# A four-layer graph network on one core: edge records padded to 72 values, degree one-hots built in pieces with waits, and one of the sorts without a wait at each operation

## The reference, cut to what matters

```python
edge_index = jnp.stack([src, dst])
h = jnp.maximum(_layernorm(x, axis=-1), 0.0)
x = x + _L0_gnn_ref(h, edge_index_t, ...)                  # attention over both directions of each edge
h = jnp.maximum(_layernorm(x, axis=-1), 0.0)
x = x + _L1_gnn_ref(h, edge_attr_64, ..., edge_index)      # two mean layers; also the mean of edge_attr_64 per node
h = jnp.maximum(_layernorm(x, axis=-1), 0.0)
x = x + _L2_gnn_ref(h, src, dst, ...)                      # mean over neighbours
h = jnp.maximum(_layernorm(x, axis=-1), 0.0)
x = x + _L3_gnn_ref(h, edge_index, ...)                    # attention with 8 heads
```

```python
deg = jax.ops.segment_sum(jnp.ones((src.shape[0],), h_e.dtype), dst, num_segments=n)
inv_deg = (1.0 / jnp.maximum(deg, 1.0))[:, None]
nbr_r = jax.ops.segment_sum(h_r, dst, num_segments=n) * inv_deg
```

## Time and profile before

| | us |
|---|---|
| median of 3 runs | 7473.32 (7467.55 to 7474.53) |
| the profiled execution | 7467.53 |
| its span | 7465.8 |
| DVE busy | 4758.9 (64%) |
| POOL busy | 4419.4 (59%) |
| PE busy | 2966.4 (40%) |
| ACT busy | 1296.9 (17%) |

### The profile page before, as it was taken

How to read it: one execution, slowest core, us unless ns; L and a number is a source line. 1 busy time by engine, 2 the same in 40 slices (tenths; PEclk the granted TensorE clock), 3 DMA queues, 4 the chain that set the end, 5 groups by cost and what they waited for, 6 DMA issues and landing times.

```text
span 7465.8 us, 65693 instructions
## 1 busy us (share of the span) xinstructions
PE 2966.4 (40%) x14101; PEld 2001.3 (27%) x14102; DVE 4758.9 (64%) x7439; ACT 1296.9 (17%) x4662; POOL 4419.4 (59%) x4260
## 2 busy tenths in 40 slices
PE   1841010110322222222222215766766467777664
PEld 0631000110212121212121213454544223233224
DVE  7998889981777777777777753333344154554544
ACT  0000000000100000000000000000000277777761
POOL 0887778887777777777777750000000477777741
PEclk6555555555555555555555556666666588888885
DMA  6112222111222222222222212424233122222211
GB/s 241 24 36 39 45 57 39 30 31 37 68 62 66 64 66 64 65 65 66 64 68 62 68 37 82 141 83 140 90 127 124 20 59 53 53 59 52 58 44 42
DMA packets 445364, 501.74 MB, mean 67 GB/s; under 512 B 233700, under 2 KB 250404, under 8 KB 440958
## 3 DMA queue, kind: packets, MB, share of 16 engines
q1 hardware_dynamic: 177882, 285.81, 11.4%
q0 software_dynamic: 140016, 139.81, 10.5%
q10 hardware_dynamic: 127284, 74.37, 3.4%
HBM read 330.98 MB, written 167.83 MB: 67 GB/s over the span
## 4 chain that ended last, share of the span: by engine, by line
POOL 54%; issue 21%; PE 13%; DVE 7%; DMA 4%; DVEq 0%; POOLq 0%; ACT 0%; ACTq 0%; SPq 0%
POOL arena L617 39%; POOL rec_dram L585 12%; PE acc L1666 9%; DVE arena L1313 2%; DMA V<-in_edge_attr_dram 2%; PE acc L1510 2%; POOL pdum L579 1%; DMA rec_dram<-V,rowst 1%; PE acc L1512 1%; POOL own_dram L603 1%; POOL arena L636 1%; PE acc L1690 0%; PE pt L1500 0%; DVE OHX L1150 0%; DVE arena L834 0%
## 5 line engine op out<-in xcount | busy, mean ns | idle before, releaser
L617 POOL DMA_INDIRECT arena<-tab_dram,jst x2976 | 2965.5, 996 | 893.6 <-issue 893.6
L585 POOL DMA_INDIRECT rec_dram<-V,rowst x800 | 1180.5, 1476 | 253.3 <-issue 245.5
L579 POOL TENSOR_TENSOR pdum<-pdum 128x1 f32<-128x1 f32 x308 | 116.2, 377 | 1698.0 <-DVE arena L1341 1363.6
L1666 PE MATMUL acc<-V,oh 128*128 x4464 | 726.0, 325 | 374.4 <-DVE arena L1313 275.3
L1313 DVE TENSOR_TENSOR arena<-arena,acc 128x192 f32 x1116 | 395.1, 354 | 639.4 <-PE acc L1666 623.3
L1666 PEld LDWEIGHTS acc<-V,oh 128*128 128x128 bf16 x4464 | 493.9, 111 | 605.9 <-issue 463.1
L745 ACT ACTIVATE arena<-arena,ew 128x64 f32<-128x64 f32 x1984 | 479.8, 333 | 88.1 <-PE acc L1690 44.3
L1150 DVE TENSOR_TENSOR OHX<-iotab,OHX 128x1024 bf16<-128x1024 bf16 x372 | 455.1, 1223 | 49.5 <-DVE OHX L1150 20.2
L745 ACT ACTIVATE OHX<-arena,ew 128x64 f32<-128x64 f32 x1984 | 479.6, 333 | 3.0
L1622 PE MATMUL pt<-OHX 128*128 128x128 bf16 x744 | 96.2, 310 | 955.4 <-DVE OHX L1150 955.4
L1622 PE MATMUL pw<-OHX 128*128 128x128 bf16 x744 | 96.1, 310 | 923.8 <-DVE OHX L1150 923.8
(11 more groups left out here) (464 smaller groups left out, 6410.3 us busy)
## 6 DMA issues: line engine op xcount, KB each, us to landing
oh<-mt_dram SPq DMA_DIRECT2D x279, 512.0 KB, 3.3
arena<-tab_dram,jst POOLq DMA_INDIRECT x2976, 2.5
mt_dram<-oh ACTq DMA_DIRECT2D x186, 256.0 KB, 2.1
rec_dram<-V SPq DMA_DIRECT2D x2, 15860.0 KB, 67.3
OHX<-rec_dram SPq DMA_DIRECT2D x122, 260.0 KB, 3.3
V<-in_edge_attr_dram ACTq DMA_DIRECT2D x100, 250.0 KB
rows_dram<-V SPq DMA_DIRECT2D x16, 1056.0 KB, 4.3
rows_dram<-arena SPq DMA_DIRECT2D x15, 1056.0 KB, 4.2
```

The costliest lines, as they stand in the source:

```text
L579: nc.gpsimd.tensor_tensor(pdum[:, 1:2], pdum[:, 0:1], pdum[:, 0:1], ALU.add).then_inc(S["pd"], 1)
L585: gp.indirect_dma_start(rec[:, :], bass.IndirectOffsetOnAxis(ap=rowst[:, q, k:k + 1], axis=0), recst[:, q, k, :], None).then_inc(S[f"scat{ ...
L617: gp.indirect_dma_start(hd.G[:, a.r, j, :], None, table[:, :], row_of(jst[:, a.r, j:j + 1])).then_inc(S[f"{x}g{a.r}"], 16)
L1666: last = nc.tensor.matmul(group_sum(g), mring[:, slot, g * 4 + k, :], hsp[:, bass.ds(rows[g * 4 + k] * (3 * D), 3 * D)], start=k == 0, sto ...
```

## The change

Three edits. First, a record has 72 values in place of 65. The seven more are set to 0 in the staging buffers once; the blank records get -1 in all eight values behind the 64. Second, `degree_ones` builds the wide one-hot in two halves of 125x1024, and the engine waits for each operation before it issues the next; there are six in place of four for a step. Third, `compare` keeps the wait between its operations for the two sorts on `SBL` only; in the sort on `SB_` one wait at the end of a step is left.

```diff
-REC = D + 1
+REC = 72
...
+            gp.memset(recst[:, :, :, D + 1:REC], 0.0).then_inc(S["blank"], 1)
...
             def degree_ones(i, q, first):
 
-                c = bass.ds((i * 2 + q) * KP, KP)
                 if not first:
                     v.wait_ge(S["dgm"], i * 2 + q - 1)
+                part = [0]
+
+                def ones_of(o, values, wide, a, n):
+
+                    k = bass.ds((i * 2 + q) * KP + a, n)
+                    V.tensor_tensor(o[:, a:a + n], iota[0:EP, 0:wide].unsqueeze(1).to_broadcast([EP, n, wide]),
+                                    values[:, k].unsqueeze(2).to_broadcast([EP, n, wide]), ALU.is_equal).then_inc(S["dg"], 1)
+                    part[0] += 1
+                    v.wait_ge(S["dg"], i * 12 + q * 6 + part[0])
                 for l in range(2):
-                    for o, k, wide in ((dhi, bkf, NC), (dlo, lof, P)):
-                        V.tensor_tensor(o[:, q, l], iota[0:EP, 0:wide].unsqueeze(1).to_broadcast([EP, KP, wide]),
-                                        k[l][:, c].unsqueeze(2).to_broadcast([EP, KP, wide]), ALU.is_equal).then_inc(S["dg"], 1)
+                    ones_of(dhi[:, q, l], bkf[l], NC, 0, KP)
+                    ones_of(dlo[:, q, l], lof[l], P, 0, KP // 2)
+                    ones_of(dlo[:, q, l], lof[l], P, KP // 2, KP // 2)
...
                     V.tensor_tensor(halves(dst, 0, 0), halves(src, 0, 0), halves(src, 1, 0), ALU.min).then_inc(S["v"], 1)
                     n[0] += 1
-                    v.wait_ge(S["v"], n[0])
+                    if bufs is SBL:
+                        v.wait_ge(S["v"], n[0])
                     V.tensor_tensor(halves(dst, 1, 0), halves(src, 0, 0), halves(src, 1, 0), ALU.max).then_inc(S["v"], 1)
...
                             V.tensor_tensor(o[r], a[r], b[r], op).then_inc(S["v"], 1)
                             n[0] += 1
-                            v.wait_ge(S["v"], n[0])
+                            if bufs is SBL:
+                                v.wait_ge(S["v"], n[0])
...
-                                RG[:, c.r, :, D:REC].to_broadcast([P, GT, P]), ALU.is_equal).then_inc(S["roh"], 1)
+                                RG[:, c.r, :, D:D + 1].to_broadcast([P, GT, P]), ALU.is_equal).then_inc(S["roh"], 1)
...
-                pe.wait_ge(S["dg"], 8 * i + 4 * q + 4)
+                pe.wait_ge(S["dg"], 12 * i + 6 * q + 6)
```

More of the change, by code:

```diff
@@ L197, in build @@
         MS = [OHXf[:, a:a + NBL * MW].rearrange("p (g x) -> p g x", x=MW) for a in (2048, 4400)]
-        lcol = V3f[:, 2200:2200 + 8 * RP]
+        lcol = V3f[:, 2304:2304 + 8 * RP]
         Dg = OHXf[0:NC, 4400:4400 + NFIL]
@@ L572, in _ @@
             gp.memset(ZF, 0.0).then_inc(S["zf"], 1)
+            gp.wait_ge(S["blank"], 3)
             gp.wait_ge(S["fill"], 16 * 2)
```

## The result

The changed kernel takes 7397.44 us (median of 4, 7395.53 to 7406.59) against 7471.79 for the kernel before (7467.55 to 7474.53, with one more run than the table above): ratio 0.9903, 95% interval 0.9886 to 0.9921. The forecast was 7418, in a range of 7375 to 7455. The profiled execution, at 7406.59, is the slowest of its four, so its gain of 61 us is smaller than the 74 of the medians.

What follows compares the result with a forecast made beforehand. The end of POOL's record scatter, paced by DVE's operations, bounds the start. DVE's +79 and -41 us are hidden, records cost 0, the scatter's end moves -55: 7473.3 - 55 = 7418 us, range 7375 to 7455.

Steps and rivals of the forecast that it cites:

- What bounds the start: Start of the kernel: everything behind 1740 us moves with the end of POOL's record scatter; DVE has 114 us of slack.
- Degree one-hots on DVE: Degree stretch: halves of 1.21 us with gaps of 0.14 take 350 us instead of 271, DVE +79 us.
- Degree one-hots on POOL: Scatters beside the degree one-hots: 178 by the end of the stretch, formerly 90.
- with holds, 1.96: Degree stretch: time for each scatter including holds, 1.96 us instead of 3.01; without holds 1.71 instead of 2.69.
- the prediction's rules: Scatter meeting a DVE operation: held until that operation ends, then needs 1.06 us; next starts 0.30 later. Unmet: 1.19.
- step by step procedure: Scatters stepped through DVE's operations: scatter end 1679.7 us, kernel before 1735.0, one-hots alone 1641.7, sort alone 1753.6.
- Sort on SB_: Sort without inner waits: DVE -41 us, ending at 1715; scatters 2.00 us each in first steps, then 2.21, formerly 1.68 and 2.17.
- the own rows: Between last scatter and first gather: 73.1 us of own rows and first loads, taken as unedited and unchanged.
- Lockout: Sort on SB_: DVE without waits keeps POOL out until the next wait; scatter end 1775, total 7510 us; chance 0.08.
- Missed gap: Degree stretch: scatters miss the 0.14 us gap, so 136 pass, not 178; scatter end 1758, total 7492 us; chance 0.07.
- Width: Record scatter: row width sets its price, so each of 800 gets 0.24 us cheaper; total about 7300 us; chance 0.07.
- No change: Record scatter: not really paced by DVE, or gains lost in other meetings; 7473 us; chance 0.08 including anything down to -35.

Runs made afterwards that it cites:

- e2: Kernel before with only the waits inside the steps of the sort on SB_ taken out: 8408 us against 8383, ratio 1.0029.
- e1: Changed kernel with the waits of the sort on SB_ put back, one-hots still in pieces: 8289 us against 8383 for the kernel before, ratio 0.9886.
- e3: Kernel before with only the records widened from 65 to 72 values: 8380 us against 8383, ratio 1.0001.
- e5: Changed kernel with the waits after the one-hot pieces removed and the sort's waits put back: 8281 us against 8345 for the kernel before, ratio 0.9923.
- e4: Kernel before with a wait after each whole degree one-hot, not cut into pieces: 8386 us against 8345, ratio 1.005.
- e1b: Second run of e1, beside the whole change on one chip: 8244 us against 8345 for the kernel before, ratio 0.9885; the change there 8287.

## Why the prediction was right, and where it was off

**What bounds the start: right.** The first gather moved by 69.8 us, the span by 61.0. In between layer 0's gathers took 4.4 us more, the part up to layer 3 2.0, layer 3's 3.6, and the tail 1.2 less: 69.8 - 4.4 - 2.0 - 3.6 + 1.2 = 61.0.

**Degree one-hots on DVE: right.** Pieces of 1.225 us (forecast 1.21), stretch up to 541.2 (536), DVE +84 (+79), hidden as forecast.

**Degree one-hots on POOL: right in mechanism, one term wrong in size.** 192 scatters, not 178. The step that erred is not the "1.71" for a scatter beside the pieces but "with holds, 1.96". Between the first and the last scatter of the stretch lie 351.0 us; 26.2 of them are what the 23 changes of set take beyond the usual 0.30, and the rest is 1.70 for each scatter. The step from 1.71 to 1.96 over 178 scatters is 44 us for the holds, 18 too many. So the prediction let a change of set cost 2.0 us, and it cost 1.14. POOL in the change, around one change of set:

```profile
334.15 1.19 POOL L587 DMA_INDIRECT rec_dram<-V,rowst  x1 [0.30 <-issue]
335.64 1.68 POOL L587 DMA_INDIRECT rec_dram<-V,rowst  x1 [0.31 <-issue]
337.63 1.20 POOL L587 DMA_INDIRECT rec_dram<-V,rowst  x1 [0.30 <-issue]
339.13 1.65 POOL L587 DMA_INDIRECT rec_dram<-V,rowst  x1 [0.30 <-issue]
340.81 0.33 POOL L581 TENSOR_TENSOR pdum<-pdum 128x1 f32<-128x1 f32 x1
341.32 0.19 POOL L581 TENSOR_TENSOR pdum<-pdum 128x1 f32<-128x1 f32 x1 [0.18 <-POOL pdum L581]
342.12 1.20 POOL L587 DMA_INDIRECT rec_dram<-V,rowst  x1 [0.61 <-issue]
```

The scatter ahead of the hold was held, the one behind it passes at once. Of the 192, 112 take less than 1.21 us: 28 of them start in a gap, 18 within the first 0.04 us of an operation, and 66 within its last 0.11 us, where the rule itself gives no more than 0.11 + 1.06. If the scatters are stepped by the prediction's rules through the measured operations of DVE, an estimate, with 0.9 to 1.1 us more at each change of set, the stretch takes 192; with 1.2 it takes 176. So the rules hold, and the count jumps with a tenth of a microsecond in the hold. The gap, 0.14 in the median, was as forecast. The prediction had such a jump of 30 us in its range, for another cause, a gap of 0.16.

In the sum: the last stretch held 134 scatters instead of 148, 31 us less at 2.21 each, and began 5 us later, so the end came 26 us before the 1680. The other 4 are those by which the step by step procedure had the kernel before too early (1735.0 for 1738.8). Together the scatter's end moved by 85.0, 30 more than the 55 of the sum.

**Sort on SB_: right in place, sign and size.** First steps: forecast 70 scatters at 2.00, measured 71 in the 141 us. Rest 2.21, measured 2.21. DVE's sort end 1715, measured 1714.6, is in part luck: the degree stretch took 5 us more than forecast and the sort 5 less (from 543.4 us to 497.7, 46 less instead of 41), mostly since a step of four takes 2.50, not 2.54. By the model e2's scatter should end 19 us after the kernel before, measured 18; e1's 93 before, in fact 127, the same degree term.

**What was missed: the own rows.** "Nothing in them is edited" was true, but they run on POOL and obey the same rule. With the scatter's end pulled ahead of the sort's end, 50 own rows of 0.96 us became 50 of 1.23 in the mean; with the transfers and loads around them the distance from last scatter to first gather grew from 73.1 to 88.3. In the kernel before they had followed DVE's sort; I took them at that length, though the change itself would move them beside the sort. This 15 us and the 30 above have opposite signs, so the first gather came 15 earlier than the forecast 1757, and the profiled span, with 61.0 for 55, looks better foreseen than its two halves were: that is luck. The medians moved by 74. e2 and e3, where the scatter still ends behind the sort, keep 0.96 and 73.0.

**Rivals.** Lockout: refuted by the timeline of the change and by e2. Missed gap: refuted, more pass than forecast, and e5 shows what no gap is worth. Width: refuted by e3. No change: refuted. The Trainium skill, page "SBUF — State Buffer", section "Who interferes with whom", infers that `tensor_tensor` leaves the descriptor work of GpSimd alone; in e4 a scatter of 2.85 us, held through a `tensor_tensor` of 2.29, contradicts that. The same section gives the block for a whole instruction where it speaks of the modes in which VectorE takes both ports, and for two SBUF inputs it says that the two contend. A hold up to the end of the one instruction is what all these rows show, but only in one direction. The prediction let the two engines block each other and took the earlier trace rows for it; there the DVE operation at 1396.63 starts inside a scatter and takes 1.23 all the same. Up to the end of the sort in the kernel before, 186 operations on 128x1024 with an indirect transfer beside them have a median of 1.225 us, 12 with none 1.226. DVE was not slowed by POOL.

## What to carry to other kernels

Where GpSimd issues transfers beside VectorE, look at how often VectorE's operations end, not at how busy it is: cut operations that are much longer than one issue, try a gap behind them where GpSimd is the later engine, and stop where the pace no longer rises (here at halves of 1.22 us). Taking out waits makes the engine that has them faster and may make its neighbour slower; ask first which of the two anybody waits for. And when a wait or a transfer moves forward, price again everything that moves with it, beside its new neighbours. Of the versions here the pieces with the sort's waits (0.9885) or with waits in the steps of four alone (0.9876) are better than the whole change; the only comparison on one chip is that of e1b.

## What the runs showed of the hardware

The gap at a loop's branch depends on where the loop lies in the engine's program: 0.5 or 3.1 us before the first operation of the same 340 recorded instructions, with a shift of two and of ten, and by the same shift of ten 3.6 or 0.6 for the 366 of layer 0's loop. The Trainium skill, page "Runtime: NRT & Kernel Launch", section "Instruction fetch mechanics", says that a taken branch whose target isn't within the two pages of instructions at hand has to wait for them to be fetched; that a body fits into them or doesn't, depending on its start, agrees with these rows.

Chips differ in the layer loops, not in the start. With the change on a chip of the second kind, VectorE's largest waits between 2500 and 4200 us:

```profile
DVE arena L1132 <- issue: 115.7, 80, 3.5
DVE OHX L1162 <- issue: 112.9, 87, 2.4
DVE arena L1146 <- issue: 109.3, 68, 3.3
```

In the change's first run the same stretch has 33.3 us in 10 waits for the first of these, all ten behind the loop's branch, and no such entry for the other two. On the chip of the second kind 9 of the waits over 0.8 us lie behind the branch and 280 behind none; their cause wasn't tried.
